# A gated Toeplitz convolution in fp32: units taken in pairs, a place of its own for each chunk of x, and another order of transfers in the last stretch

## The chip, the core and the metric

One NeuronCore of a Trainium2 chip runs the whole program. TensorE (PE in the profile) multiplies, ScalarE (ACT) and VectorE (DVE) empty PSUM and do the pointwise work, GpSimd (POOL) does pointwise work on SBUF, and SyncE (SP) issues every DMA of this kernel from one in-order queue. The metric is device time in microseconds, the median of three runs: 815.77 us before (814.77 to 816.03).

## What is computed

With x of shape (8, 64, 64, 96) in float32, `srms` dividing each token by the root of its mean square, and `toep1`, `toep2` the two causal-and-anticausal convolutions whose 127 coefficients per channel come from small networks of four layers (written as FFTs of double length in the reference):

```python
xn  = srms(x)
u   = silu(xn @ u_w.T + u_b)                  # 288 channels
v   = silu(xn @ v_w.T + v_b)                  # 288 channels
out = toep2(v, along rows) + toep1(v, along columns)
return (u * out) @ o_w.T + o_b + x
```

## The kernel before, in words

The 8 images are two halves of four. A half has 32 steps of 512 tokens. The program has five stages, in this order:

- **Phase A** (0 to about 175 us): for each step of half 0, the x of that step is scaled by its norm (`scale`, POOL), transposed (`transpose_x`, PE), split into a high and a low part (ACT, DVE), and multiplied by the two weight matrices (`project`, PE). ACT applies silu; v stays in SBUF, u is stored to DRAM by SP (`store_u`). x comes in 8 chunks of 4 steps (`load_x_all`). POOL squares a chunk two chunks ahead of its use (`square_a0`), DVE sums it and makes the norms. Chunks 0 to 3 lie in rows of v that are still free, chunks 4, 5, 6 in the three tiles `x_late`, and chunk 7 in the first of these again.
- **Phase C for half 0** (to about 325 us): the convolution, in 36 units of 8 channels. For unit n, PE transposes v into the PSUM banks 4 and 5 (`transpose_v`), multiplies along columns with 64x64 tiles (`along_columns`, 16 instructions, line 1034) and along rows with 128x128 tiles (`along_rows`, 8 instructions, line 1049). The sums of unit n lie in banks 0 and 1 for even n, 2 and 3 for odd n. ACT copies the transposed v to SBUF (`evacuate_vt`, line 591) and the result back into v (`evacuate_y`, lines 597 and 602). DVE writes the Toeplitz matrices of unit n + 2 from a staged tile that SP loads (`toeplitz`, lines 826 and 832; `load_stage`). In half 0 DVE also makes the norms of half 1 there.
- **Phase B0** (to about 538 us): the output of half 0, step by step, together with the projections of half 1.
- **Phase C for half 1** (to about 690 us).
- **Phase B1** (to the end): the output of half 1. For step t, SP has loaded u into one of four places (`load_u`), POOL multiplies it by the convolved v (`gate`, line 504), PE transposes the product in three parts (`transpose_g`, line 984) and, one step behind, multiplies by the output weights (`project_out`, lines 994 and 997), DVE adds x, which SP has loaded into the tile `x_e1` (`load_xe`, `add_x`), and SP stores that tile (`store_out`). `x_e1` has four places too.

Each engine runs its instructions in the order of the code, and waits on semaphores where one engine needs another. Two such waits matter below. `transpose_v(n)` waits for `vt_ready`, the copy of the unit before, since all units share banks 4 and 5; `along_columns(n)` waits for all three parts of `evacuate_y(n - 2)`. In phase B1 `load_xe` waits for `o_stored`, the landing of the store that last used its place.

Of the kernel before, what the change touches and what calls it, by code (L numbers as in the profile page):

```python
# [32 lines left out]
IMAGES, HEIGHT, WIDTH, E = 8, 64, 64, 96  # L33
D = 288
RPE, LAYERS = 256, 3
EPS = 1e-8
P = 128
H = P // 2
NB = 4
STEPS = HEIGHT // 2  # L40
# [3 lines left out]
NCH = 3  # L44
# [3 lines left out]
UNITS = D // UNIT  # L48
RC = RPE // P
TOK = NB * P  # L50
CH = 4
CHUNKS = STEPS // CH
PAIRS = 4
# [5 lines left out]
def tno_kernel(nc, x, x_eT, u_wT, u_b, v_wT, v_b, o_wT, o_b, pos_w, pos_b, lwT, lb, out_wT, out_b, out):  # L59
# [7 lines left out]
    with ctx:  # L67
# [3 lines left out]
        def place(name, shape, offset, dtype=f32):  # L71
            return nc.alloc_sbuf_tensor_at(name, shape, dtype, offset=base + offset)
# [6 lines left out]
        free_rows = place("free_rows", [P, D // 2, 2, P], 0)  # L79
# [4 lines left out]
        CHUNK_ROWS = CH * NB  # L84
# [3 lines left out]
        OB = OW + 2 * RC * NCH  # L88
        RH = OB + 2 * NCH
        RSQ, RIN, W_RAW = RH + 2 * RC, RH + 4 * RC, RH + 6 * RC  # L90
        assert W_RAW + 2 * NCH <= D // 2

        def lw_row(n, o, layer, c):
            return LW + ((n * RC + o) * LAYERS + layer) * RC + c
# [6 lines left out]
        V = V_BYTES  # L101
# [10 lines left out]

        g = place("g", [P, 5, TOK], V + 36864, f32r)
        g1 = [place(f"g1{k}", [P, 5, TOK], V + 26624 + 12288 * k, f32r) for k in range(2)]
        x_late = [place(f"x_late{k}", [P, CHUNK_ROWS, E], V + offset) for k, offset in enumerate((36864, 13824, 0))]

        def x_chunk(c):

            if c < FREE_CHUNKS:
                return rows(CHUNK_ROWS * c, CHUNK_ROWS, E)  # L120
            return x_late[(c - FREE_CHUNKS) % 3][:]

        x_n = place("x_n", [P, CH * NB, E], V + 22528)

# [108 lines left out]
        def _(sp):  # L233
# [10 lines left out]
            def load_x_all(c):  # L244
                wait(sp, x_all_loaded, 32 * c)
                for i in range(2):
                    sp.dma_start(x_chunk(c)[H * i:H * i + H], rows_of(0, CH * c, CH, i)).then_inc(x_all_loaded, 16)
# [50 lines left out]
            def load_xe(half, t, r):  # L298
                k = r % (2, CH)[half]
                sp.dma_start((x_e, x_e1)[half][:, k].rearrange("e (s m) -> e s m", s=2), tokens_of(x_eT, half, t)  # L300
                             ).then_inc(xe_loaded[half][k], 16)

            def store_out(half, t, r):
                k = r % (2, CH)[half]
                sp.wait_ge(o_ready, STEPS * half + t + 1)
                sp.dma_start(tokens_of(out, half, t), (x_e, x_e1)[half][:, k].rearrange("e (s m) -> e s m", s=2)
                             ).then_inc(o_stored[half][k], 16)
# [11 lines left out]
                                 ).then_inc(stage_loaded[k], 16)  # L319

            def phase_a(c, first, last):
                if c + 3 < CHUNKS - 1:
                    load_x_all(c + 3)
                elif c + 2 == CHUNKS - 1:

                    sp.wait_ge(x_scaled, CH * (c + 2 - 2))
                    load_x_all(c + 2)
                for r in range(CH):
                    if last and r == 2:
                        sp.wait_ge(a_stored, 32)  # L330
                        for n in range(2):
                            load_stage(0, n)
                    store_u(0, CH * c + r, u_tile(0, r), ua_stored[r % 2])
# [63 lines left out]
            def phase_b1():  # L397
                def body(c, first, last):
                    for r in range(CH):
                        t = CH * c + r  # L400
                        if not (first and r == 0) and not (last and r > 0):
                            sp.wait_ge(y_transposed, NCH * STEPS + NCH * t)
                            load_u(1, t + 3, r + 3)
                        if not (first and r < CH - 1) and not (last and r == CH - 1):
                            up = (r + 1) // CH
                            sp.wait_ge(o_stored[1][(r + 1) % CH], 16 * c + 16 * up)
                            load_xe(1, t + 1, r + 1)
                        if not first or r >= 2:
                            store_out(1, t - 2, r + 2)
                for c in range(CHUNKS):  # L410
                    body(c, c == 0, c == CHUNKS - 1)
                for t in range(STEPS - 2, STEPS):
                    store_out(1, t, t)
# [126 lines left out]
        def _(act):  # L540
# [45 lines left out]
            def phase_c(half):  # L586
                def evacuate_vt(n):
                    N = UNITS * half + n
                    act.wait_ge(vt_transposed, N + 1)
                    wait(act, conv_done, N - 1)  # L590
                    nc.scalar.copy(vt[n % 2][:], ps[:, VT_BANK:VT_BANK + 2].rearrange("p b (c m) -> p (b c) m", m=P)  # L591
                                   ).then_inc(vt_ready, 1)

                def evacuate_y(n):
                    act.wait_ge(conv_done, UNITS * half + n + 1)
                    bank, pair, pairs = SET_BANK[n % 2], UNIT // 2 * n, UNIT // 4
                    nc.scalar.copy(v[:, pair:pair + pairs],  # L597
                                   ps[:, bank].rearrange("p (c e m) -> p c m e", e=2, m=P)).then_inc(conv_out, 1)

                    for i in range(2):  # L600
                        to, of = slice(H * i, H * i + H), slice(H - H * i, P - H * i)
                        nc.scalar.copy(v[to, pair + pairs:pair + 2 * pairs],  # L602
                                       ps[of, bank + 1].rearrange("p (c e m) -> p c m e", e=2, m=P)
                                       ).then_inc(conv_out, 1)

                evacuate_vt(0)
                for n in range(UNITS):
                    if n:
                        evacuate_y(n - 1)
                    if n + 1 < UNITS:  # L610
                        evacuate_vt(n + 1)
                    elif half == 0:
                        high_x(STEPS, 0)
                evacuate_y(UNITS - 1)

            def body0(c, first, last):
                for r in range(CH):
# [304 lines left out]
        def _(pe):  # L922
# [93 lines left out]
            def phase_c(half):  # L1016
                def transpose_v(n):
                    N = UNITS * half + n
                    wait(pe, vt_ready, N)
                    for c in range(UNIT):  # L1020
                        last = nc.tensor.transpose(ps[:, VT_BANK + c // NB, (c % NB) * P:(c % NB + 1) * P],  # L1021
                                                   v[:, UNIT // 2 * n + c // 2, :, c % 2], (ident, swap)[c // NB][:])
                    last.then_inc(vt_transposed, 1)
# [27 lines left out]
                                                start=False, stop=True, skip_group_check=True)  # L1051
                    last.then_inc(conv_done, 1)

                pe.wait_ge(silu_done, PAIRS * STEPS * (half + 1) - 2)
                transpose_v(0)
                for n in range(UNITS):
                    if n < 2:
                        pe.wait_ge(silu_done, PAIRS * STEPS * (half + 1) - 1 + n)
                    along_columns(n)
                    if n + 1 < UNITS:  # L1060
                        transpose_v(n + 1)
                    elif half == 0:
                        transpose_x(STEPS, 0)
                    along_rows(n)

            def body0(c, first, last):
                for r in range(CH):
# [83 lines left out]
```

## Time and profile before

| | |
|---|---|
| median of 3 runs | 815.77 us (814.77 to 816.03) |
| profiled execution | 814.11 us |
| its span | 812.3 us |
| PE busy | 749.5 us (92%) |
| ACT, DVE, POOL busy | 533.9, 470.2, 282.6 us |
| granted TensorE clock, mean | 0.989 |
| DMA queue of SP | 160.15 MB, 70.6% of 16 engines |

The span goes from the first instruction to the last; the device time of the same execution is 1.8 us longer. Busy time says little here by itself: a stage in which PE is busy all the time and a stage in which a transfer sets the pace lie next to each other, and the page's forty slices of 20.3 us show it (PE reads 9 tenths in nearly all of them, and 8 or 7 in most of the last six, which are phase B1). "Idle before, released by" behind an instruction names what it waited for last.

### The profile page before, as it was taken

Reading aid. Unit: us, or ns where it says so; the run is one execution under the profiler, and the core shown is the slowest. Engines: PE = TensorE matmul, PEld = TensorE weight load, DVE = VectorE, ACT = ScalarE, POOL = GpSimd, SP = SyncE. Lnnn points to the kernel's source line nnn. Section 1 sums busy time; section 2 is a strip of 40 time slices with the busy share of each in tenths; the row PEclk is TensorE's granted clock in tenths of the full one; section 3 lists DMA queues with packets and bytes.
Section 4 is the critical chain, followed back from the end, with each engine's and each line's share of the span. In section 5 each row is a group of like instructions: output and inputs, shape, how many; then the busy total and the mean of one; then the engine's idle time right before and its main releaser. Section 6 shows DMA issues by size and latency. Waiting matters only on the chain.

```text
span 812.3 us, 19208 instructions
## 1 busy us (share of the span) xinstructions
PE 749.5 (92%) x7148; PEld 672.2 (83%) x7148; DVE 470.2 (58%) x845; ACT 533.9 (66%) x866; POOL 282.6 (35%) x187
## 2 busy tenths in 40 slices
PE   0999997998999999899999999989999998987887
PEld 0999886988999998799999999979999998765655
DVE  6566542336898886444444454445455553776666
ACT  0566574775666666677777877746666666655554
POOL 4333333212212112655555555410000001966764
PEclk9999998999999999999999999989999999999999
DMA  9555554369889786488988888776555555688786
GB/s 209 159 156 156 156 134 138 160 199 215 187 193 200 160 187 191 144 272 272 270 271 262 266 275 271 231 202 144 133 134 131 136 134 185 200 250 248 247 262 193
DMA packets 132017, 161.11 MB, mean 198 GB/s; under 512 B 69484, under 2 KB 97132, under 8 KB 131948
## 3 DMA queue, kind: packets, MB, share of 16 engines
q1 hardware_dynamic: 131948, 160.15, 70.6%
q8 instruction: 48, 0.79, 0.4%
q14 instruction: 21, 0.17, 0.1%
HBM read 109.49 MB, written 50.63 MB: 197 GB/s over the span
## 4 chain that ended last, share of the span: by engine, by line
PE 75%; DMA 13%; DVE 4%; issue 2%; POOL 2%; SPq 2%; ACT 1%; ACTq 0%; DVEq 0%; POOLq 0%
PE ps L974 22%; PE ps L1049 15%; PE ps L1021 9%; PE ps L1034 9%; DMA out<-x_e 9%; PE ps L994 7%; PE ps L984 6%; PE ps L965 3%; DMA stage<-a_dram 2%; PE ps L997 1%; POOL u_in L504 1%; DMA u_dram<-u_in 1%; SPq L300 1%; PE ps L948 1%; DMA free_rows<-in_x 1%
## 5 line engine op out<-in xcount | busy, mean ns | idle before, releaser
L504 POOL TENSOR_TENSOR u_in<-u_in,v 128x1152 f32<-128x1152 f32 (+2 forms) x66 | 174.6, 2651 | 177.5 <-DMA u_in<-u_dram 161.0
L876 DVE TENSOR_TENSOR g<-ps,g 128x512 fp32r<-128x512 f32 (+1 forms) x192 | 125.7, 681 | 74.9 <-ACT g L571 45.8
L832 DVE COPY toepB<-stage 64x512 f32<-64x512 f32 x144 | 105.2, 730 | 80.1 <-PE ps L1049 72.6
L1049 PE MATMUL ps<-toepB,vt 128*128 128x128 f32 x1152 | 141.8, 277 | 0.9 <-POOL toepB L488 0.5
L1049 PEld LDWEIGHTS ps<-toepB,vt 128*128 128x128 f32 x1152 | 136.3, 194 | 1.4 <-POOL toepB L488 0.7
L974 PE MATMUL ps<-wu,xh 97*128 97x288 f32 x512 | 123.6, 307 | 2.1
L766 DVE TENSOR_TENSOR xl<-ps,xh 96x512 fp32r<-96x512 f32 x64 | 43.9, 687 | 140.5 <-ACT xh L544 140.5
L974 PE MATMUL ps<-wv,xh 97*128 97x288 f32 x512 | 120.8, 311 | 2.3 <-ACT u_in L548 1.3
L984 PE MATMUL ps<-ident,u_in 128*128 128x128 f32 (+1 forms) x768 | 102.2, 276 | 21.3 <-POOL u_in L504 20.3
L984 PEld LDWEIGHTS ps<-ident,u_in 128*128 128x128 f32 (+1 forms) x768 | 81.7, 127 | 36.8 <-DVE g L876 12.7
L548 ACT ACTIVATE v<-ps 128x576 f32 (+1 forms) x128 | 83.5, 652 | 38.2 <-PE ps L974 28.7
L994 PE MATMUL ps<-g,wo 128*96 128x512 f32 x384 | 101.8, 400 | 0.0
L567 ACT CAST g<-ps 128x512 fp32r<-128x512 f32 x128 | 68.9, 590 | 47.8 <-PE ps L984 47.6
L591 ACT COPY vt<-ps 128x1024 f32<-128x1024 f32 x72 | 72.9, 1012 | 39.8 <-PE ps L1021 39.8
L974 PEld LDWEIGHTS ps<-wu,xh 97*128 97x128 f32 x512 | 89.1, 190 | 11.3 <-issue 3.7
L974 PEld LDWEIGHTS ps<-wv,xh 97*128 97x128 f32 x512 | 88.0, 193 | 3.5 <-ACT u_in L548 1.6
L548 ACT ACTIVATE u_out<-ps 128x576 f32<-128x576 f32 x96 | 62.6, 652 | 41.3 <-PE ps L974 39.5
L1034 PE MATMUL ps<-v,toepA 64*64 64x128 f32 x2304 | 82.9, 280 | 5.6 <-DVE toepA L826 5.6
L602 ACT COPY v<-ps 64x512 f32<-64x512 f32 x144 | 83.6, 581 | 3.6
L597 ACT COPY v<-ps 128x512 f32<-128x512 f32 x72 | 42.2, 586 | 59.0 <-PE ps L1049 59.0
L1034 PEld LDWEIGHTS ps<-v,toepA 64*64 64x64 f32 x2304 | 64.8, 132 | 14.4 <-issue 4.0
L974 PE MATMUL ps<-wv,xl 97*128 97x288 f32 x256 | 76.7, 300 | 0.0
(79 smaller groups left out, 1006.5 us busy)
## 6 DMA issues: line engine op xcount, KB each, us to landing
stage<-a_dram SPq DMA_DIRECT2D x144, 256.0 KB, 4.3
u_in<-u_dram SPq DMA_DIRECT2D x64, 576.0 KB, 5.3
u_dram<-u_out SPq DMA_DIRECT2D x48, 576.0 KB, 3.3
x_e<-in_x_eT SPq DMA_DIRECT2D x64, 192.0 KB, 3.8
out<-x_e SPq DMA_DIRECT2D x64, 192.0 KB, 3.8
u_dram<-u_in SPq DMA_DIRECT2D x16, 576.0 KB, 2.8
x_n<-in_x SPq DMA_DIRECT2D x16, 384.0 KB, 5.4
xa<-in_x SPq DMA_DIRECT2D x64, 96.0 KB, 4.6
```

What stands on the lines that cost most here:

```text
L504: return nc.gpsimd.tensor_tensor(out=tile, in0=tile, in1=v[:, start // 2:end // 2, bass.ds(t * NB, NB)].rearrange("p c n e -> p n c e"), o ...
L548: nc.scalar.activation(target, source, ACT.Silu).then_inc(silu_done, 1)
L591: nc.scalar.copy(vt[n % 2][:], ps[:, VT_BANK:VT_BANK + 2].rearrange("p b (c m) -> p (b c) m", m=P)).then_inc(vt_ready, 1)
L602: nc.scalar.copy(v[to, pair + pairs:pair + 2 * pairs], ps[of, bank + 1].rearrange("p (c e m) -> p c m e", e=2, m=P)).then_inc(conv_out, 1)
L832: nc.vector.tensor_copy(toepB[n % 2][rows, :, rows], stage[n % STAGES][rows, axis].rearrange("p k c -> p c k")[:, :, ::-1]).then_inc(toepB ...
L876: nc.vector.tensor_tensor(out=low, in0=ps[0:w, bank], in1=high.bitcast(f32), op=ALU.subtract).then_inc(gl_ready, 1)
L974: last = nc.tensor.matmul(ps[:, n, 0:D], (xh, xl)[xp][r % 2][:, n * P:(n + 1) * P], w[:, wp], start=(k == 0), stop=(k == len(SPLIT) - 1))
L984: last = nc.tensor.transpose(columns[:, n // 2, n % 2], u_in[:, r % CH, n, k * P:k * P + KW[k]], ident[:])
L994: nc.tensor.matmul(ps[0:E, bank], wo[:, 2 * k + wp], tile[:, 2 * k + gp], start=(k + s == 0), stop=False)
L1021: last = nc.tensor.transpose(ps[:, VT_BANK + c // NB, (c % NB) * P:(c % NB + 1) * P], v[:, UNIT // 2 * n + c // 2, :, c % 2], (ident, swap ...
L1034: last = nc.tensor.matmul(ps[to, SET_BANK[n % 2] + b, c * P:(c + 1) * P], toepA[n % 2][of, ch], v[of, UNIT // 2 * n + ch // 2, :, ch % 2], ...
L1049: last = nc.tensor.matmul(ps[:, SET_BANK[n % 2] + c // NB, (c % NB) * P:(c % NB + 1) * P], vt[n % 2][:, c], toepB[n % 2][:, c], start=Fals ...
```

## The change

Three edits, with no instruction of arithmetic added or taken away.

1. **Phase C.** PE takes the units two by two: both `along_columns`, then for each of the two `along_rows` and `transpose_v` of the unit two further on. The first two transposes come ahead of everything, and the wait for the last silus is one wait before them. ACT begins with two `evacuate_vt` and then alternates `evacuate_y(n)`, `evacuate_vt(n + 2)`.
2. **Phase A.** Chunk 4 of x goes to another free region of rows of v, chunks 5, 6, 7 to the three `x_late` tiles. No place is used twice, the wait on `x_scaled` is gone, and chunk 7 is loaded at the start of chunk 4, where before it was loaded at the start of chunk 5.
3. **Phase B1.** In the body of step t SP issues the load of u(t + 3), then the store of the output t - 2, then the load of x(t). Before it was u(t + 3), x(t + 1), output t - 2.

```diff
         def x_chunk(c):
             if c < FREE_CHUNKS:
                 return rows(CHUNK_ROWS * c, CHUNK_ROWS, E)
-            return x_late[(c - FREE_CHUNKS) % 3][:]
+            if c == FREE_CHUNKS:
+                return free_rows[:, X_FREE:X_FREE + CHUNK_ROWS, 1, P - E:P]
+            return x_late[c - FREE_CHUNKS - 1][:]
...
             def phase_a(c, first, last):
-                if c + 3 < CHUNKS - 1:
+                if c + 3 < CHUNKS:
                     load_x_all(c + 3)
-                elif c + 2 == CHUNKS - 1:
-                    sp.wait_ge(x_scaled, CH * (c + 2 - 2))
-                    load_x_all(c + 2)
...
                             load_u(1, t + 3, r + 3)
-                        if not (first and r < CH - 1) and not (last and r == CH - 1):
-                            up = (r + 1) // CH
-                            sp.wait_ge(o_stored[1][(r + 1) % CH], 16 * c + 16 * up)
-                            load_xe(1, t + 1, r + 1)
                         if not first or r >= 2:
                             store_out(1, t - 2, r + 2)
+                        if not first:
+                            sp.wait_ge(o_stored[1][r], 16 * c)
+                            load_xe(1, t, r)
...
-                evacuate_vt(0)
+                for n in range(2):
+                    evacuate_vt(n)
                 for n in range(UNITS):
-                    if n:
-                        evacuate_y(n - 1)
-                    if n + 1 < UNITS:
-                        evacuate_vt(n + 1)
-                    elif half == 0:
+                    evacuate_y(n)
+                    if n + 2 < UNITS:
+                        evacuate_vt(n + 2)
+                    elif half == 0 and n == UNITS - 2:
                         high_x(STEPS, 0)
-                evacuate_y(UNITS - 1)
...
-                pe.wait_ge(silu_done, PAIRS * STEPS * (half + 1) - 2)
-                transpose_v(0)
-                for n in range(UNITS):
-                    if n < 2:
-                        pe.wait_ge(silu_done, PAIRS * STEPS * (half + 1) - 1 + n)
-                    along_columns(n)
-                    if n + 1 < UNITS:
-                        transpose_v(n + 1)
-                    elif half == 0:
-                        transpose_x(STEPS, 0)
-                    along_rows(n)
+                pe.wait_ge(silu_done, PAIRS * STEPS * (half + 1))
+                for n in range(2):
+                    transpose_v(n)
+                for n in range(0, UNITS, 2):
+                    for k in range(2):
+                        along_columns(n + k)
+                    for k in range(2):
+                        along_rows(n + k)
+                        if n + 2 + k < UNITS:
+                            transpose_v(n + 2 + k)
+                        elif half == 0 and k == 0:
+                            transpose_x(STEPS, 0)
```

TensorE inside phase C, before. `toepA` belongs to the products along columns, `toepB` and `vt` to those along rows, `ident` and `swap` to the transposes; x16, x8 and x4 are instructions in a row.

```order
L1034 MATMUL ps<-v_49,toepA1_72 64x128 x16
L1021 MATMUL ps<-ident_90,v_49 128x128 x4
L1021 MATMUL ps<-swap_91,v_49 128x128 x4
L1049 MATMUL ps<-toepB1_74,vt1_76 128x128 x8
L1034 MATMUL ps<-v_49,toepA0_71 64x128 x16
L1021 MATMUL ps<-ident_90,v_49 128x128 x4
L1021 MATMUL ps<-swap_91,v_49 128x128 x4
L1049 MATMUL ps<-toepB0_73,vt0_75 128x128 x8
```

And after the change, at the same place:

```order
L1032 MATMUL ps<-v_49,toepA0_71 64x128 x16
L1032 MATMUL ps<-v_49,toepA1_72 64x128 x16
L1047 MATMUL ps<-toepB0_73,vt0_75 128x128 x8
L1019 MATMUL ps<-ident_90,v_49 128x128 x4
L1019 MATMUL ps<-swap_91,v_49 128x128 x4
L1047 MATMUL ps<-toepB1_74,vt1_76 128x128 x8
L1019 MATMUL ps<-ident_90,v_49 128x128 x4
L1019 MATMUL ps<-swap_91,v_49 128x128 x4
```

Two units have two groups of 64x64 products in both; after the change these stand together, and the products along rows of the first unit have a transpose and the rows of the second right behind them.

SyncE in phase A, from the middle on, before. `x_late0` is the place of chunk 7, `a_dram` takes the convolution's coefficients.

```order
L277 DMA a_dram<-r_a_78 128x36x8 [waits a_ready]
L277 DMA a_dram<-r_a_78 128x36x8
L295 DMA u_dram<-u_in_51 128x1152 [waits silu_done]
L295 DMA u_dram<-u_out_60 128x1152 [waits silu_done]
L295 DMA u_dram<-u_in_51 128x1152 [waits silu_done]
L295 DMA u_dram<-u_out_60 128x1152 [waits silu_done]
L247 DMA x_late0_64<-in_x 64x16x96 [waits x_all_loaded,x_scaled]
```

After the change chunk 7 is in `x_late2`:

```order
L281 DMA a_dram<-r_a_78 128x36x8 [waits a_ready]
L281 DMA a_dram<-r_a_78 128x36x8
L251 DMA x_late2_66<-in_x 64x16x96 [waits x_all_loaded]
L251 DMA x_late2_66<-in_x 64x16x96
L299 DMA u_dram<-u_in_51 128x1152 [waits silu_done]
L299 DMA u_dram<-u_out_60 128x1152 [waits silu_done]
L299 DMA u_dram<-u_in_51 128x1152 [waits silu_done]
```

The load moved ahead of four stores of u; it now stands between the store of the coefficients and the store of u of step 16.

SyncE in phase B1, before, for a little more than a step. The digit at the end of `o_stored` is the place in `x_e1`.

```order
L306 DMA out_0<-x_e1_53 96x2x256 [waits o_ready]
L290 DMA u_in_51<-u_dram 128x1152 [waits y_transposed]
L300 DMA x_e1_53<-in_x_eT 96x2x256 [waits o_stored10]
L306 DMA out_0<-x_e1_53 96x2x256 [waits o_ready]
L290 DMA u_in_51<-u_dram 128x1152 [waits y_transposed]
```

And after:

```order
L294 DMA u_in_51<-u_dram 128x1152 [waits y_transposed]
L310 DMA out_0<-x_e1_53 96x2x256 [waits o_ready]
L304 DMA x_e1_53<-in_x_eT 96x2x256 [waits o_stored13]
L294 DMA u_in_51<-u_dram 128x1152 [waits y_transposed]
L310 DMA out_0<-x_e1_53 96x2x256 [waits o_ready]
```

The load of x before waited for the store issued one step earlier (t + 1 and t - 3 share a place); now it waits for the store issued two steps earlier (t and t - 4 share one).

## Rows read from the trace of the kernel before

**Rows 1.** Windows; columns: stretch, length, busy PE, PEld, DVE, ACT, POOL, PEclk, DMA share, GB/s.
```profile
375.00:380.00 5.00, 5.00 (x35) 4.54 (x35) 3.02 (x5) 3.78 (x7) 3.38 (x2) 1.00 1.01 325
340.00:540.00 200.00, 198.24 (x1420) 180.84 (x1418) 94.23 (x149) 156.61 (x271) 99.51 (x58) 1.00 0.83 258
713.00:788.00 75.00, 60.89 (x371) 44.67 (x369) 51.82 (x79) 41.45 (x80) 50.77 (x20) 1.00 0.80 251
```

**Rows 2.** Timeline of SyncE in phase B1: start, length, instruction (all us).
```profile
717.11 0.45 SPq L306 DMA_DIRECT2D out<-x_e  x1
...
720.81 0.32 SPq L300 DMA_DIRECT2D x_e<-in_x_eT  x1
721.17 0.45 SPq L306 DMA_DIRECT2D out<-x_e  x1
```

**Rows 3.** Timeline of PE in phase B1, the output products.
```profile
698.39 1.64 PE L994 MATMUL ps<-g,wo 128*96 128x512 f32 x6
...
701.33 1.64 PE L994 MATMUL ps<-g,wo 128*96 128x512 f32 x6
...
805.37 1.64 PE L994 MATMUL ps<-g,wo 128*96 128x512 f32 x6
```

**Rows 4.** Transfers issued from 713 to 788 us: count, size, median us to landing.
```profile
u_in<-u_dram SPq DMA_DIRECT2D x19, 576.0 KB, 5.5
x_e<-in_x_eT SPq DMA_DIRECT2D x20, 192.0 KB, 3.4
```

**Rows 5.** Timeline of PE in phase A; in brackets idle time before it and releaser.
```profile
116.53 0.40 PE L974 MATMUL ps<-wv,xh 97*128 97x288 f32 x1 [1.32 <-ACT u_in L548]
...
120.47 0.38 PE L974 MATMUL ps<-wv,xh 97*128 97x288 f32 x1
...
129.81 1.09 PE L965 MATMUL ps<-ident,xa 128*96 128x128 f32 x4 [5.61 <-POOL xa L443]
...
136.25 0.38 PE L974 MATMUL ps<-wv,xh 97*128 97x288 f32 x1
```

**Rows 6.** Timeline of POOL in phase A.
```profile
128.14 0.83 POOL L456 TENSOR_TENSOR x_sq<-x_late 128x384 f32<-128x384 f32 x1 [15.70 <-DMA x_late<-in_x]
```

**Rows 7.** Timeline of SyncE in phase A.
```profile
108.22 3.38 SPq L295 DMA_DIRECT2D u_dram<-u_in  x1
...
121.43 1.60 SPq L247 DMA_DIRECT2D x_late<-in_x  x2
```

**Rows 8.** Timeline of ACT in phase A.
```profile
115.82 1.19 ACT L548 ACTIVATE u_in<-ps 128x576 f32<-128x576 f32 x2 [2.18 <-DMA u_dram<-u_in]
```

**Rows 9.** Timeline of PE's weight loads over one unit of phase C.
```profile
603.02 1.88 PEld L1049 LDWEIGHTS ps<-toepB,vt 128*128 128x128 f32 x16
605.02 0.89 PEld L1034 LDWEIGHTS ps<-v,toepA 64*64 64x64 f32 x32
606.09 0.55 PEld L1021 LDWEIGHTS ps<-ident,v 128*128 128x128 f32 x4 [0.18 <-issue]
...
607.03 0.31 PEld L1049 LDWEIGHTS ps<-toepB,vt 128*128 128x128 f32 x2
```

**Rows 10.** Timeline of ACT over the same unit.
```profile
605.13 0.59 ACT L597 COPY v<-ps 128x512 f32<-128x512 f32 x1 [0.77 <-PE ps L1049]
605.74 1.19 ACT L602 COPY v<-ps 64x512 f32<-64x512 f32 x2
607.35 1.01 ACT L591 COPY vt<-ps 128x1024 f32<-128x1024 f32 x1 [0.42 <-PE ps L1021]
```

**Rows 11.** Timeline of PE where the phases C and B1 start.
```profile
190.74 1.14 PE L1034 MATMUL ps<-v,toepA 64*64 64x128 f32 x32 [1.78 <-DVE toepA L826]
...
542.10 1.98 PE L1034 MATMUL ps<-v,toepA 64*64 64x128 f32 x32 [3.86 <-DVE toepA L826]
...
690.92 2.19 PE L984 MATMUL ps<-ident,u_in 128*128 128x128 f32 x12 [2.51 <-POOL u_in L504]
```

**Rows 12.** Timeline of DVE in phase C of half 0.
```profile
231.55 3.78 DVE L832 COPY toepB<-stage 64x512 f32<-64x512 f32 x2 [0.76 <-PE ps L1049]
```

More of the change, by code:

```diff
@@ L90, in tno_kernel @@
         RSQ, RIN, W_RAW = RH + 2 * RC, RH + 4 * RC, RH + 6 * RC
-        assert W_RAW + 2 * NCH <= D // 2
+        X_FREE = W_RAW + 2 * NCH
+        assert X_FREE + CHUNK_ROWS <= D // 2
         def lw_row(n, o, layer, c):
@@ L114, in tno_kernel @@
         g1 = [place(f"g1{k}", [P, 5, TOK], V + 26624 + 12288 * k, f32r) for k in range(2)]
-        x_late = [place(f"x_late{k}", [P, CHUNK_ROWS, E], V + offset) for k, offset in enumerate((36864, 13824, 0))]
+        x_late = [place(f"x_late{k}", [P, CHUNK_ROWS, E], V + offset) for k, offset in enumerate((0, 13824, 36864))]
         def x_chunk(c):
```

## The prediction, made before the changed kernel had run

> **What bounds the kernel now.** I read the windows by stage first. In phase B0 TensorE is busy 198.24 of 200 us, in phase B1 60.89 of 75 us, and no other engine is full there [rows 1]. So the stages differ, and each edit has to be priced in its own stage.
>
> Phase B1: SP's timeline shows what sets the step. The store of one output is issued at 717.11, the next load of x at 720.81, and 0.36 us later the next store, at 721.17 [rows 2]. The load of x waits for the landing of the store before it, the next store stands behind the load of x, so store, landing (3.7 us), load, store is a circle of 4.06 us a step. The output products of TensorE show the same: 698.39 to 701.33, or 2.94 us a step, while the places are still full, but 104.04 us for the 28 steps from 701.33 to 805.37, 3.72 us a step [rows 3].
>
> Phase A: TensorE idles 5.61 us ahead of the transpose at 129.81 [rows 5], since POOL waited 15.70 us for chunk 7 of x [rows 6], which SP issued only at 121.43 [rows 7].
>
> Phase C: TensorE is never idle over the unit shown. From 603.02 to 607.03 its weight loads follow each other, 4.01 us a unit [rows 9], while ACT waits 0.77 and 0.42 us [rows 10].
>
> **Phase B1, step by step.** The work of a step on TensorE is unchanged, so its floor is 2.94 us. The load of x now waits for the store issued two steps earlier. The old circle then spans two steps and no longer binds: 3.7 us of landing in two steps. Is there another circle? The load of x of step t goes out behind the store of t - 2; it must land (3.4 us in the median [rows 4], from 713 to 788), DVE adds, the store of t goes out, then the load of t + 2: about 3.4 + 1.3 us for two steps, 2.35 a step; even with 5 us of landing it is 3.15. For u: transposes of t - 1 done, u lands 5.5 us later [rows 4], then POOL's gate and the transposes of t + 3, some 10.2 us in four steps, 2.55 a step. Neither circle binds before the data rate does. A step moves 576 KB of u, 192 KB of x and 192 KB of output, 983,040 bytes. At 2.94 us this would be 334 GB/s. B1 runs at 251 GB/s with a DMA share of 0.80; B0 holds 258 GB/s over 200 us, where TensorE sets the pace, and its best 5 us move 325 GB/s at a share of 1.01 [rows 1]. So the pace comes out between 2.94 us (TensorE) and 3.81 us (258 GB/s), and nearest to the row in which the engines were full: 325 GB/s gives 3.02, with some gaps I take 312 GB/s, 3.15 us. The first five steps stay at 2.94 us as the places are full. Then 5 x 2.94 + 23 x 3.15 = 87.2 us in place of 104.0, a gain of **16.9 us**; bounds 1.7 (3.81 us) and 21.7 (2.94 throughout). The last load of x goes out a step later than before, but the last products of TensorE hide most of its landing, so I put nothing for it.
>
> The Trainium skill (DMA: Bandwidth & Descriptors, Specifications) gives a limit from HBM of about 358 GB/s for a core. By it the step would need 2.75 us of transfer and TensorE would set the pace, with the full 21.7 us; no row here shows such a rate over 5 us.
>
> **Phase A.** A step of four projections takes 3.94 us when nothing waits (116.53 to 120.47); the two steps from 120.47 to 136.25 took 15.78 us [rows 5], the lower clock after the idle time included. With chunk 7 loaded a chunk earlier the whole 7.9 us go. But the load moves to a bad place: right behind the store of the coefficients in runs of 32 bytes, which holds up the issue of the next store of u for 3.38 us [rows 7]. That store lands late already: ACT waits 2.18 us for it at 115.82 [rows 8], and TensorE 1.3 us behind ACT [rows 5]. Now 384 KB of x stand ahead of it. At least this costs nothing, at most the 3.4 us that the store was held up; I take 1.5 us. Then TensorE idles 3 us there. At 690.92 an idle time of 2.51 us was followed by 12 transposes in 2.19 us [rows 11]. Four transposes of phase C have their weight loads done in 0.55 us [rows 9], so 12 take some 1.5 at the higher level: the granted clock had fallen from 2.4 to 1.2 GHz. In phase A the lower level after 129.81 makes 7.9 us out of 5.61 us of idle time, 2.3 us more; after a shorter idle time I add 1.7 us. Phase A gains 7.9 - 1.5 - 1.7 = **4.7 us**; bounds 7.9 - 3.4 - 1.7 = 2.8 and 7.9.
>
> **Phase C.** A unit has one change from 128x128 to 64x64 products and one back. Weight loads of the row products start every 0.113 us (1.88 us for 16, the last one's own 0.19 off), so without a change the next would start at 603.02 + 1.80; it starts at 605.02, 0.20 later [rows 9]. The 32 loads of the 64x64 products need 0.80 us by their own spacing, and the transpose starts 1.07 after the first, 0.27 later [rows 9]. Taken by two, one such pair of changes goes in every two units: 8.03 becomes 7.56 us.
>
> But ACT now comes into the circle. Let the row products of unit n start at 0. ACT's copy of the result starts 2.11 later (603.02 to 605.13) and ends at 3.91; the copy of vt takes 1.01, so the banks of the transposes are free at 4.95 [rows 9, 10]. TensorE wants them for the transpose of n + 3 at 1.80 + 0.94 + 1.80 = 4.54, since two row products and one transpose are all that lies between. Before, a whole unit lay between. So it waits 0.44 us: 5.0 + 0.94 (transpose) + 0.20 + 2 x 0.80 + 0.27 = 8.0 us for two units in place of 8.03. The other new wait, of the second column products for the second copy of the result, ends at 6.8 where TensorE arrives at 6.9, and costs nothing. The saving of the changes is eaten by the wait. I take 7.98; the spacing of the 64x64 loads leaves 7.87 to 8.10.
>
> The rest of phase C: the last pair of a half needs no transpose and keeps its saving, 1.1 us in half 1 and 0.9 in half 0. At the start of half 0 the matrix of unit 3 isn't ready until 190.74 [rows 11], and in the new order the row products of unit 2 stand behind this wait instead of ahead of it: -2.2 us. In half 1 the transposes of unit 1 move into the wait that ends at 542.10 [rows 11], which pays for the later start. DVE in half 0 is nearly full, and its matrix for unit n + 3 now has 2.8 us of room where it had 5.8; a pair of its copies sometimes takes 3.78 us [rows 12] and eats most of it: -1 us. Sum: 31 x 0.05 + 2.0 - 2.2 - 1.0 = **+0.4 us**; bounds -5 (8.10 and more waits on DVE) and +5 (7.87).
>
> The Trainium skill (TensorEngine Tiling (Array Packing), Tiling Modes) says that changing the tiling mode drains TensorE. The gaps of 0.20 and 0.27 us agree. By that rule alone the edit would be worth 36 x 0.47 = 17 us; it doesn't look at who empties PSUM.
>
> **Sum.** 16.9 + 4.7 + 0.4 = 22.0 us against the profiled execution: 814.1 - 22.0 = 792.1. The median of the runs is 1.7 above that execution, so 793.7.
>
> **The rivals.**
> - TensorE sets the pace of B1, 2.94 us a step. For it: the circles above leave room, and single stretches reach 325 GB/s. Against it: 334 GB/s would have to hold for 80 us. It gives 793.7 - 4.8 = 788.9.
> - The transfers give less: with small packets of x and output between the large ones they stay near 270 GB/s, 3.6 us a step. For it: B0 averages 258 GB/s. Against it: there TensorE set the pace. 14.7 + 82.8 us is a gain of only 6.5: 804.1.
> - The pairs save all their changes of mode, 7.56 us for two units, because the wait on vt doesn't show. 31 x 0.42 = 13 us more: 780.7. Against it stands ACT's timeline.
> - The load of chunk 7 doesn't help, because POOL and DVE are late by themselves: 793.7 + 4.7 = 798.4. Against it: POOL idles 15.70 us there.
> - Slower: DVE becomes the bound of phase C in half 0. Its copies of the matrices come in the order rows n, columns n + 3, rows n + 3, with the norms between them; if a stretched copy (3.78 us) delays the columns of unit n + 3 in most pairs, TensorE waits up to 1.5 us in each of 17 pairs, and all later pairs inherit it. It takes 22 us, 1.3 us a pair, to undo the rest; at 1.5, 25.5 us: 819.2. Against it: in the rows POOL's long squares, which go with the stretched copies, come once in four units.
>
> **How the numbers follow.** Forecast 0.60, TensorE sets the pace 0.14, less from the transfers 0.12, all changes saved 0.06, chunk 7 without effect 0.04, slower 0.04. The forecast's 793.7, with the pace of B1 from 3.02 to 3.3 us and phase C at its bounds, covers about 787 to 800. The range of 783 to 806 takes in the rivals but the slower one and most of the one with all changes saved. Faster than before by over 0.2% (about 1.6 us, what a measurement can tell from no change) 0.93; within it 0.03, where the slowest end of the transfers meets the worst of phase C; slower 0.04.
>
> **What the profile of the changed kernel would show.** In B1 SP no longer waits for a landed store ahead of the load of x, the output products start every 3.0 to 3.3 us, the DMA share is over 0.9 and the rate over 300 GB/s. In phase A no idle time of TensorE near 124 us, a longer one near 115. In phase C two units take 8.0 us, and the second transpose of each pair waits about 0.4 us for the copy of vt. I am wrong if the B1 rate stays under 280 GB/s, if TensorE is full there, or if two units take under 7.8 or over 8.3 us.

## The result

| | before | after |
|---|---|---|
| median | 815.27 us (4 runs, 812.87 to 816.03) | 791.81 us (4 runs, 791.14 to 794.66) |
| profiled execution | 814.11 us | 791.14 us |
| its span | 812.3 us | 789.3 us |
| PE busy | 749.5 us (92%) | 740.7 us (94%) |
| DMA queue of SP | 160.15 MB, 70.6% | 160.15 MB, 72.2% |

The ratio is 0.9724, with a 95% interval of 0.9692 to 0.9756. The forecast was 793.7 us. It came within 1.9 us, but two of its three terms were off, in opposite directions, and the runs below sort them out.

I cut each profiled execution at four places: the start of the last product of phase A, the end of the last row products of each phase C, and the start of the last output product of phase B0. That gives the length of each stage in us (rounded one by one).

| | A | C0 | B0 | C1 | B1 and end | span |
|---|---|---|---|---|---|---|
| before | 174.8 | 148.5 | 213.7 | 151.5 | 123.9 | 812.3 |
| after | 170.1 | 151.3 | 213.8 | 151.8 | 102.5 | 789.3 |
| gain | 4.7 | -2.8 | -0.1 | -0.2 | 21.4 | 23.0 |
| predicted | 4.7 | -1.5 | 0 | 1.9 | 16.9 | 22.0 |

(The prediction gave phase C as one sum, 0.4; its terms are put to their halves here.)

### The profile page after: what moved, and what is told of

It is laid out like the page before. It is cut to its first block, busy times and chain, and to the rows that moved or that the text cites. A ratio compares the mean times of both kernels' runs of the same rounds, so it can differ in the third digit from the quotient of the medians.

```text
span 789.3 us, 19203 instructions
## 1 busy us (share of the span) xinstructions
PE 740.7 (94%) x7148; PEld 672.7 (85%) x7148; DVE 472.6 (60%) x845; ACT 530.2 (67%) x866; POOL 280.6 (36%) x187
## 3 DMA queue, kind: packets, MB, share of 16 engines
q1 hardware_dynamic: 131948, 160.15, 72.2%
## 4 chain that ended last, share of the span: by engine, by line
PE 74%; ACT 11%; issue 4%; DMA 4%; DVE 4%; POOL 1%; SPq 1%; POOLq 0%; ACTq 0%; DVEq 0%
PE ps L972 24%; PE ps L992 10%; PE ps L982 10%; PE ps L1047 9%; PE ps L1032 9%; ACT v L601 5%; PE ps L1019 5%; ACT vt L590 4%; PE ps L963 3%; PE ps L995 2%; DMA stage<-a_dram 2%; POOL u_in L503 1%; DMA u_in<-u_dram 1%; DMA u_dram<-u_in 1%; PE ps L946 1%
## 5 line engine op out<-in xcount | busy, mean ns | idle before, releaser
L503 POOL TENSOR_TENSOR u_in<-u_in,v 128x1152 f32<-128x1152 f32 (+2 forms) x66 | 174.6, 2653 | 155.0 <-DMA u_in<-u_dram 137.7
L1047 PE MATMUL ps<-toepB,vt 128*128 128x128 f32 x1152 | 144.9, 279 | 0.0
L830 DVE COPY toepB<-stage 64x512 f32<-64x512 f32 x144 | 99.7, 693 | 55.9 <-PE ps L1047 48.9
L972 PE MATMUL ps<-wv,xh 97*128 97x288 f32 x512 | 119.0, 308 | 5.3 <-ACT u_in L547 4.0
L982 PEld LDWEIGHTS ps<-ident,u_in 128*128 128x128 f32 (+1 forms) x768 | 83.5, 128 | 13.4 <-ACT v L601 2.7
L1032 PE MATMUL ps<-v,toepA 64*64 64x128 f32 x2304 | 76.2, 279 | 2.4 <-DVE toepA L824 2.4
L824 DVE COPY toepA<-stage 128x512 f32<-128x512 f32 x72 | 48.5, 674 | 46.8 <-PE ps L1032 28.9
L972 PE MATMUL ps<-wu,xl 97*128 97x288 f32 x256 | 76.1, 297 | 0.0
```

Of the source, the lines that this page charges most:

```text
L503: return nc.gpsimd.tensor_tensor(out=tile, in0=tile, in1=v[:, start // 2:end // 2, bass.ds(t * NB, NB)].rearrange("p c n e -> p n c e"), o ...
L830: nc.vector.tensor_copy(toepB[n % 2][rows, :, rows], stage[n % STAGES][rows, axis].rearrange("p k c -> p c k")[:, :, ::-1]).then_inc(toepB ...
L972: last = nc.tensor.matmul(ps[:, n, 0:D], (xh, xl)[xp][r % 2][:, n * P:(n + 1) * P], w[:, wp], start=(k == 0), stop=(k == len(SPLIT) - 1))
L982: last = nc.tensor.transpose(columns[:, n // 2, n % 2], u_in[:, r % CH, n, k * P:k * P + KW[k]], ident[:])
L1032: last = nc.tensor.matmul(ps[to, SET_BANK[n % 2] + b, c * P:(c + 1) * P], toepA[n % 2][of, ch], v[of, UNIT // 2 * n + ch // 2, :, ch % 2], ...
L1047: last = nc.tensor.matmul(ps[:, SET_BANK[n % 2] + c // NB, (c % NB) * P:(c % NB + 1) * P], vt[n % 2][:, c], toepB[n % 2][:, c], start=Fals ...
```

## The profile after

Windows of the changed kernel (stretch, length, busy PE, PEld, DVE, ACT, POOL, PEclk, DMA share, GB/s), two stretches of 5 us in phase A and one of 75 us in B1:

```profile
115.00:120.00 5.00, 1.54 (x9) 1.54 (x10) 0.55 (x1) 1.98 (x4) 0.00 (x0) 0.95 0.71 265
120.00:125.00 5.00, 5.00 (x30) 4.99 (x30) 2.13 (x3) 2.90 (x6) 3.06 (x4) 0.71 0.24 99
...
700.00:775.00 75.00, 75.00 (x483) 60.15 (x482) 66.52 (x103) 53.77 (x103) 68.05 (x26) 1.00 1.00 325
```

The last row answers to the last of [rows 1]. TensorE was busy 60.89 of 75 us and is now busy for all 75; the rate went from 251 to 325 GB/s. So in this trace B1 isn't bound by its transfers, as I had forecast, but by TensorE.

**Phase B1.** The output products in TensorE's timeline:

```profile
731.95 1.64 PE L992 MATMUL ps<-g,wo 128*96 128x512 f32 x6
...
734.89 1.64 PE L992 MATMUL ps<-g,wo 128*96 128x512 f32 x6
...
737.83 1.64 PE L992 MATMUL ps<-g,wo 128*96 128x512 f32 x6
```

SyncE's timeline in the same stretch:

```profile
732.06 0.32 SPq L310 DMA_DIRECT2D out<-x_e  x1
732.43 0.45 SPq L304 DMA_DIRECT2D x_e<-in_x_eT  x1
732.92 0.48 SPq L294 DMA_DIRECT2D u_in<-u_dram  x1
734.95 0.32 SPq L310 DMA_DIRECT2D out<-x_e  x1
```

The step is 2.94 us, the floor of TensorE read from [rows 3]. The load of x goes out 0.37 us after the store ahead of it, where it stood 3.7 us behind before [rows 2]. SyncE's waits over B1 say it for the whole stretch (line, what it waited for, us in total, times, longest). Before, from 700 to 800 us:

```profile
SPq L300 <- DMA out<-x_e: 66.1, 26, 3.0
```

And after, from 700 to 775 us:

```profile
SPq L310 <- DVE x_e L883: 38.1, 25, 2.1
SPq L294 <- PE ps L982: 0.9, 2, 0.5
```

Before, 26 loads of x waited for a landed store, 2.5 us each. After, none does: SyncE waits for DVE to finish an output.

**Phase A.** The stall at chunk 7 is gone, and one near 115 us is longer. TensorE's timeline there, after the change:

```profile
118.46 0.40 PE L972 MATMUL ps<-wv,xh 97*128 97x288 f32 x1 [3.98 <-ACT u_in L547]
```

ACT's timeline, the instruction that TensorE waited for:

```profile
117.76 1.19 ACT L547 ACTIVATE u_in<-ps 128x576 f32<-128x576 f32 x2 [4.84 <-DMA u_dram<-u_in]
```

And SyncE's, ahead of it:

```profile
103.35 4.14 SPq L281 DMA_DIRECT2D a_dram<-r_a  x2
107.53 4.16 SPq L251 DMA_DIRECT2D x_late<-in_x  x2
111.73 0.97 SPq L299 DMA_DIRECT2D u_dram<-u_in  x1
```

The two loads of chunk 7 now stand where the store of u stood before, right behind the store of the coefficients, and take 4.16 us to issue, as that store took 3.38 [rows 7]; further on in the queue, in [rows 7], two such loads take 1.60. The store of u stands behind them. ACT goes on at 117.76, 1.9 us later than at 115.82 [rows 8], and TensorE's idle time grows from 1.32 to 3.98 us. The granted clock is at 0.71 of full speed from 120 to 125 us, a mix of its two levels, 1.2 and 2.4 GHz.

**Phase C.** TensorE's weight loads over a pair of units:

```profile
601.82 1.86 PEld L1047 LDWEIGHTS ps<-toepB,vt 128*128 128x128 f32 x16 [0.18 <-issue]
...
604.55 1.88 PEld L1047 LDWEIGHTS ps<-toepB,vt 128*128 128x128 f32 x16
606.79 0.56 PEld L1019 LDWEIGHTS ps<-ident,v 128*128 128x128 f32 x4 [0.37 <-ACT vt L590]
...
607.95 1.81 PEld L1032 LDWEIGHTS ps<-v,toepA 64*64 64x64 f32 x64
609.93 0.74 PEld L1047 LDWEIGHTS ps<-toepB,vt 128*128 128x128 f32 x6 [0.18 <-issue]
```

ACT's timeline beside them:

```profile
603.91 0.59 ACT L596 COPY v<-ps 128x512 f32<-128x512 f32 x1 [2.54 <-PE ps L1047]
604.52 1.18 ACT L601 COPY v<-ps 64x512 f32<-64x512 f32 x2
605.73 1.01 ACT L590 COPY vt<-ps 128x1024 f32<-128x1024 f32 x1
```

A pair takes 609.93 - 601.82 = 8.11 us, and two units took 8.02 [rows 9]. The wait on the copy of vt is there, 0.37 us long (0.44 was forecast): ACT ends that copy at 606.74, and the second transpose of the pair starts at 606.79.

## The experiments

Ten kernels ran. Ratios are to the kernel before on the same chip, with 95% intervals. Distances from the changed kernel are differences of medians that were taken at different times; taken from the ratios they differ by up to 2 us, so smaller ones say little. Where it matters the lengths of the stages are given too.

**Which edit brings what.** `e1_b1_only` is the kernel before with edit 3 alone, `e2_pairs_only` with edit 1 alone, and `e3_no_pairs` is the changed kernel with edit 1 undone. The core of e1 (e2 and e3 add and take away the last two pieces of the diff of the change):

```diff
-                        if not (first and r < CH - 1) and not (last and r == CH - 1):
-                            up = (r + 1) // CH
-                            sp.wait_ge(o_stored[1][(r + 1) % CH], 16 * c + 16 * up)
-                            load_xe(1, t + 1, r + 1)
...
+                        if not first:
+                            sp.wait_ge(o_stored[1][r], 16 * c)
+                            load_xe(1, t, r)
```

> The kernel before with the third edit alone (order of SP in phase B1). Theory: the circle store, landing, load of x, store is gone and TensorE sets the pace, 2.94 us a step; 812.3 - 21.4 = 790.9 us of span, ratio 0.974. Rival (the forecast's own: the transfers set the pace at 312 GB/s): 3.15 us a step, 795.4 us of span. Rival (part of the gain in B1 comes from the stages ahead of it): less than 20 us.

> The kernel before with the first edit alone (units of the convolution in pairs). Theory: a pair takes 8.11 us instead of 8.03 and the start of phase C in half 0 is later; 3 us slower, ratio 1.004. Rival (forecast): 0.4 us faster, ratio 1.000. Rival (the pairs gain, and what phase C lost in the changed kernel comes from chunk 7's place or the shifted phase A): ratio below 0.999.

> The changed kernel with the first edit undone: the units one by one as before, with both other edits. Theory: 3 us faster than the changed kernel, span 786, ratio to before 0.968. Rival: 0.4 us slower than the changed kernel, ratio 0.973.

Measured: e1 791.07 us (0.9684, 0.9657 to 0.9711), e2 820.01 (1.0041, 1.0027 to 1.0054), e3 789.21 (0.9667, 0.9644 to 0.9691). Edit 3 alone brings 25 us, all that the change brings (22.2 between the two traces, 19.9 of them in B1 and the end). Edit 1 alone makes the kernel slower by 3.3 us (by the ratio), and leaving it out of the change makes that 2.6 us faster by the medians, 4.6 by the ratios. The stages say the same. The five kernels in this study with edit 1 and nothing else new in phase C (after, e2, e4, e5, e9) need 302.6 us for C0 and C1 together in the mean, the three without it (before, e1, e3) 299.8: edit 1 costs 2.8 us. Cut once more inside phase C, at the ends of the row products of the third pair of units, of the 17th and of the last (means, us), the traces show where:

| | C0: to the third pair | next 14 pairs | last pair | C1: to the third pair | next 14 pairs | last pair |
|---|---|---|---|---|---|---|
| without edit 1 | 29.48 | 112.37 | 7.44 | 31.04 | 112.37 | 7.07 |
| with edit 1 | 30.04 | 113.59 | 7.59 | 30.64 | 113.59 | 7.16 |

The columns of 14 pairs are the same to 0.05 us in all traces of a row: 8.11 us a pair against 8.03. So 2.4 of the 2.8 us are the 28 pairs in the middle.

For edit 2 the end of phase A tells more than the medians: 174.8, 174.6 and 173.1 us without it (before, e2, e1) against 170.1, 170.7, 170.1, 171.3, 171.4 and 171.9 with it (after, e3, e4, e6, e7, e9), a gain of 3.2 us between the means. Single traces with the same code up to there differ by almost 1.9 us, and the clock goes with it: from 115 to 125 us its mean is 0.83 of full speed in after and e4 (both 170.1) and 0.66 in e3, e6, e7 and e9 (170.7 to 171.9). The 4.7 us come from one of the two traces with the higher clock.

**Order or distance in B1.** In `e4_x_first` the load of x stands ahead of the store, but still waits for the store of two steps earlier.

```diff
-                        if not first or r >= 2:
-                            store_out(1, t - 2, r + 2)
                         if not first:
...
                             load_xe(1, t, r)
+                        if not first or r >= 2:
+                            store_out(1, t - 2, r + 2)
```

> The changed kernel with one thing altered in phase B1: SP issues u(t + 3), then x(t), then the store of t - 2; the load of x still waits for the store of t - 4, issued two steps earlier. Theory: the distance to the store that is waited for matters, not the order of the two transfers; 2.94 us a step, the same time as the changed kernel, ratio 0.972. Rival: the order matters (stores ahead of loads); the pace goes back towards 3.7 us and the span to 805 or more.

Measured: 792.55 us (0.9709, 0.9674 to 0.9744). Its window:

```profile
720.00:770.00 50.00, 49.95 (x315) 38.55 (x312) 42.92 (x67) 35.38 (x68) 44.33 (x17) 1.00 1.05 320
```

The window of the changed kernel over the same stretch:

```profile
720.00:770.00 50.00, 50.00 (x324) 40.19 (x323) 44.26 (x69) 35.76 (x69) 45.97 (x18) 1.00 1.03 333
```

TensorE is full in both. SyncE's waits of e4 from 700 to 775 us show that it does wait for landed stores again:

```profile
SPq L304 <- DMA out<-x_e: 31.6, 23, 1.9
SPq L310 <- DVE x_e L883: 12.4, 15, 1.6
```

They are shorter, 1.4 us each where they were 2.5 before, and nearly fit into the step: the 30 steps of e4 take 3.01 us in the mean, against 2.96 in the changed kernel, 3.66 in the kernel before and 2.97 to 3.17 in the seven other kernels with edit 3 and no added bytes. The rival had put e4 back towards 3.7. What counts is how many steps lie between a store and the load that waits for it; what the order of the two adds can't be told from the scatter.

**How near the transfers are to being the bound.** `e9_more_bytes` adds one load of 192 KB a step to B1, into memory nobody reads, 20% more bytes.

```diff
+                        if not first:
+                            wait(sp, junk_loaded[t % 2], 16 * ((t - CH) // 2))
+                            sp.dma_start(junk[:, t % 2].rearrange("e (s m) -> e s m", s=2), tokens_of(x_eT, 1, t)
+                                         ).then_inc(junk_loaded[t % 2], 16)
```

> The changed kernel; in phase B1 SP issues one more load of 192 KB per step from step 4 on, into a place that nobody reads, so a step moves 1,179,648 bytes instead of 983,040. Theory: 333 GB/s in B1 is TensorE's pace and close to what the transfers can give, so with 20% more bytes they set the pace: 3.45 to 3.6 us a step, 28 steps, 14 to 18 us slower than the changed kernel, ratio to before 0.989 to 0.995. Rival (there is room left): up to 400 GB/s at 2.94 us a step, the same time as the changed kernel.

Measured: 809.49 us (0.9949, 0.992 to 0.9979), 17.7 us slower than the changed kernel by the medians; its ten runs lie between 806.48 and 816.59. Its window:

```profile
720.00:785.00 65.00, 56.78 (x344) 41.29 (x343) 45.84 (x72) 37.98 (x73) 48.46 (x19) 1.00 1.06 329
```

The loads of u in that stretch (count, size, median us from issue to landing):

```profile
u_in<-u_dram SPq DMA_DIRECT2D x18, 576.0 KB, 7.3
```

And in the changed kernel, from 720 to 770 us:

```profile
u_in<-u_dram SPq DMA_DIRECT2D x17, 576.0 KB, 5.7
```

With more bytes the rate doesn't rise over the 333 GB/s of after: it is 329, TensorE idles 13% of the stretch, and the loads of u land 1.6 us later. It isn't a new circle in the queue: in this stretch SyncE waits 18 times for DVE and 15 times for TensorE, and never for a landing. So here the transfers do set the pace, and 1,179,648 bytes at 329 GB/s are 3.59 us a step; 18 loads in 65 us are 3.61. The changed kernel needs 983,040 bytes in 2.94 us, 334 GB/s, and gets it. It sits right at the edge: TensorE needs 2.94 us a step, and 983,040 bytes at the 329 to 333 GB/s of the two windows take 2.95 to 2.99. The Trainium skill (DMA: Bandwidth & Descriptors, Specifications) gives about 358 GB/s for a core. Its direction was right, TensorE does set the pace, and my 312 was too low; but this case reached 325 to 333 over 50 us and more, not 358.

**Chunk 7 away from the short runs.** `e5_x7_early` is the changed kernel with the load of chunk 7 issued ahead of the coefficients' store, and that store split over two steps.

```diff
-                if c + 3 < CHUNKS:
+                if c + 3 < CHUNKS and c != LAYERS + 1:
...
+                    if c == LAYERS + 1 and r < 2:
+                        store_a(r)
...
-                    store_a()
+                    load_x_all(c + 3)
```

> The changed kernel; in phase A SP issues the load of chunk 7 ahead of the store of the coefficients, and the two halves of that store one step apart, each just ahead of a store of u. Theory: the 3.98 us of idle time of TensorE ahead of 118.46 and the lower clock after it come from the store of u that stands behind both; they go, and phase A ends 4 to 5.5 us sooner; some 1 to 2 us of it may be lost again at the start of phase C, which waits for loads. Ratio to before 0.966 to 0.968. Rival: another engine is late there (POOL, DVE) and TensorE waits for it instead; ratio as for the changed kernel, 0.972.

Measured: 791.33 us (0.9698, 0.9676 to 0.972), no difference by the medians, where 4 to 5.5 us were expected. TensorE's timeline at the stall:

```profile
116.28 0.61 PE L974 MATMUL ps<-wv,xh 97*128 97x288 f32 x1 [2.04 <-ACT u_in L549]
```

The window around it:

```profile
115.00:120.00 5.00, 3.72 (x15) 3.72 (x16) 2.35 (x2) 2.65 (x5) 0.24 (x1) 0.59 0.83 243
```

The idle time went from 3.98 to 2.04 us, but the granted clock fell all the same, to a mean of 0.59 over these 5 us. The split store holds the issue behind each of its halves instead of once: the two stores of u behind them take 4.54 and 3.38 us to issue, so the cost is moved more than removed. Phase A ended at 169.3, 170.0 and 168.2 us in the three kernels with this edit (e5, e8, e10), against 170.9 in the mean of the six that have edit 2 without it, so it is worth about 1.7 us there, as little as the traces can tell.

**The wait on vt taken away.** `e6_vt_banks` is the changed kernel with the transposed v of odd units in PSUM banks 6 and 7, which are free in phase C (the two `pe.wait_ge` that this takes at the ends of the phase, and one copy of DVE moved ahead, are not shown).

```diff
-        VT_BANK = 4
+        VT_BANK = [4, 6]
...
-                    wait(pe, vt_ready, N)
+                    wait(pe, vt_ready, N - 1)
```

> The changed kernel; the transposes of v use PSUM banks 4 and 5 for even units and 6 and 7 for odd ones (and DVE adds the last x of half 0 ahead of the first matrix of half 1, so that bank 7 is free). Nothing else. Theory: the wait of 0.4 us in each pair for the copy of vt goes, but ACT's second copy of the result then ends 0.2 us after TensorE wants it; a pair takes 7.9 us instead of 8.11, 34 pairs, 7 us faster than the changed kernel. Rival (only the wait on vt matters): 7.7 us a pair, 14 us faster. Rival (the pair is bound elsewhere): no change.

Measured: 786.0 us (0.9638, 0.9618 to 0.9657), 5.8 us faster than the changed kernel. TensorE's weight loads:

```profile
604.72 0.89 PEld L1032 LDWEIGHTS ps<-v,toepA 64*64 64x64 f32 x32
605.77 0.92 PEld L1032 LDWEIGHTS ps<-v,toepA 64*64 64x64 f32 x32 [0.17 <-issue]
606.87 1.86 PEld L1047 LDWEIGHTS ps<-toepB,vt 128*128 128x128 f32 x16 [0.18 <-ACT vt L590]
```

The transpose no longer waits, but the second group of column products now starts 0.17 us late: ACT's copies of the results alternate with the copies of vt, and the last part of the copy that it waits for ends at 605.66, 0.11 us before it starts. A pair takes 7.84 us. `e7_rows_first` takes e6 and puts both row products ahead of both transposes, and in ACT both copies of results ahead of both copies of vt:

```diff
                     evacuate_y(n)
-                    if n + 2 < UNITS:
-                        evacuate_vt(n + 2)
...
+                    evacuate_y(n + 1)
+                    for k in range(2):
+                        if n + 2 + k < UNITS:
+                            evacuate_vt(n + 2 + k)
...
                         along_rows(n + k)
-                        if n + 2 + k < UNITS:
-                            transpose_v(n + 2 + k)
...
+                    for k in range(2):
+                        if n + 2 + k < UNITS:
+                            transpose_v(n + 2 + k)
```

> As the kernel with two places for the transposes, and TensorE does both row products of a pair before both transposes, ACT both copies of the result before both copies of vt. Theory: no wait is left, a pair takes TensorE's own 7.7 us; 14 us faster than the changed kernel in half 1, somewhat less in half 0 if DVE, which has some 15 us of work in four units there, gets in the way; ratio to before 0.956. Rival (the saved changes of mode were never there): a pair takes 8.0 or more.

Measured: 783.55 us (0.9599, 0.9579 to 0.9619). TensorE over a pair:

```profile
602.06 2.05 PE L1034 MATMUL ps<-v,toepA 64*64 64x128 f32 x64
604.04 3.84 PE L1049 MATMUL ps<-toepB,vt 128*128 128x128 f32 x32
607.72 0.64 PE L1021 MATMUL ps<-ident,v 128*128 128x128 f32 x4
...
609.73 0.46 PE L1034 MATMUL ps<-v,toepA 64*64 64x128 f32 x8
```

The pair takes 7.67 us with no idle time of the matmuls, and C0 and C1 are 146.4 and 145.4 us long, together 11.2 us less than in the changed kernel. The whole is 8.3 us faster, short of the 14 expected: in this trace phase A is 1.3 and B1 2.3 us longer than in that of the changed kernel. The Trainium skill (TensorEngine Tiling (Array Packing), Tiling Modes) says that a change of mode drains TensorE. By that rule alone pairing saves 0.47 us in two units, from 8.02 to 7.55; e7 has 7.67, so 0.35 of it is there once nobody waits for PSUM. Nearly all of the missing 0.12 lies in the column products: the two groups together take 604.04 - 602.06 = 1.98 us, against 2 x 1.07 apart [rows 9], a saving of 0.16 where 0.27 had been counted.

**All of it.** `e8_all` is e7 with the edit of e5. `e10_norms_later` also puts the first load of the norms behind that of matrix 3 at the start of C0:

```diff
-                    sp.wait_ge(ua_stored[1], 16 * (STEPS // 2))
-                    load_norms(0)
                 for n in range(STAGES, UNITS):
                     load_stage(half, n)
+                    if half == 0 and n == STAGES:
+                        sp.wait_ge(ua_stored[1], 16 * (STEPS // 2))
+                        load_norms(0)
```

> The last one (rows first, two places for the transposes) together with the early load of chunk 7 and the split store of the coefficients. Theory: both gains add, 3 to 5 us below the kernel with rows first; ratio to before 0.951. Rival: what phase A gains is lost at the start of phase C; the same time as with rows first.

> The kernel with all of it (rows first, two places for the transposes, early chunk 7, split store); at the start of phase C in half 0 SP issues the load of the first x for the norms behind that of matrix 3 instead of ahead of it. Theory: the column products of unit 3 wait for that matrix, whose load stands behind 1.4 us of issue and 384 KB; 1 to 2 us faster, ratio to before 0.952 to 0.954. Rival: DVE, which needs the squares at unit 2, holds up the next matrices; same or slower.

Measured: e8 778.51 us (0.9546, 0.9522 to 0.957), e10 777.55 (0.954, 0.9519 to 0.9562). Both beat the kernel before by 37 to 38 us and the changed one by 13 to 14. Of the 5.3 us between the traces of e7 and e8 only 1.4 lie in phase A, where the edit is; 1.5 lie in phase C and 2.4 in B1, where nothing was changed. e8 and e10 aren't told apart by their times. In its trace e10 has C0 2.5 us shorter than e8 (143.5 against 146.0), as expected of the edit, and B1 with the end 7.1 us longer (109.6 against 102.5), though nothing was changed there; that trace is of its slowest run, 781.51 us. Its window:

```profile
695.00:770.00 75.00, 71.83 (x455) 55.67 (x454) 60.43 (x95) 50.05 (x96) 63.38 (x24) 1.00 0.97 303
```

e8 has TensorE busy for 74.87 us and 316 GB/s there. In e10 the loads of u land after 6.3 us (median, 700 to 770 us), in e8 after 5.7. So B1 scatters with what the transfers give, as a stage at the edge would; what slows them in some executions stays open.

## Why the prediction was right, and where not

- **Phase B1, the term mis-sized.** I put 3.15 us a step and 16.9 us; it was 2.94, and the stage gained 21.4. The circle of store, landing, load and store was read rightly, and so was the floor. The step that failed is "with some gaps I take 312 GB/s": I took the best 5 us of a stretch in which TensorE set the pace, less some gaps, for what the transfers can do. TensorE at 2.94 us was my first rival, priced at 788.9; 21.4 is within 0.3 us of its 21.7. But the stage runs at the edge, and in the nine kernels with edit 3 and no added bytes a step takes 2.96 to 3.17 us, 3.02 in the mean. By the means of the stages, 125.2 us for before and e2 and 104.3 for the nine, the gain is 20.9.
- **Phase C, wrong in sign.** I put +0.4; edit 1 costs 2.8 us. The wait on vt was read rightly: rows to transpose takes 4.97 us where I had 5.0, and transpose to columns 1.16 where I had 1.14. Four terms failed. The column products of a pair, "2 x 0.80" and 0.27, were to take 1.87 us; they take 1.98 (607.95 to 609.93), in e7 too, where nothing waits. My own sum gave 8.0 to 8.01 us, of which I took 7.98; the pair takes 8.11, so in place of 31 x 0.05 = +1.6 the 28 pairs in the middle cost 2.4. The last pairs were to keep 2.0 us and lose 0.24, for the second transpose of the pair before, with its wait, still stands ahead of their products. The start of half 0 was to cost 2.2 and costs 0.6, and that of half 1 gains 0.4. DVE was to cost 1.0 in half 0 and costs nothing: the 14 pairs take 113.59 us in both halves. These add up to the -2.8.
- **Phase A, right by the traces, 4.7 us.** The stall goes, and one of 3.98 us (I had 3) takes part of it back, with the clock. Over nine kernels the gain is 3.2, so the term was probably 1.5 too large, and that the two traces give 4.7 is luck of the clock; it lies within my bounds of 2.8 to 7.9.
- **The total** was within 1.9 us since +4.5 in B1 and -3.4 in phase C nearly cancel, and that is luck: a forecast that fits by its sum is no proof of its terms. Inside phase C the errors cancelled in part as well. Of my signs of being wrong one came true, TensorE is full in B1. It needed e2 and e3 to see that the kernel is faster without the pairs as they were written, and e6 and e7 to see that the pairs were worth having.

## What to carry to other kernels

A store, its landing and a load that waits for it in one in-order queue set a step of their own length; put two steps between them and the circle goes, whatever the order in the queue. When instructions are grouped to save changes of mode, look at who empties the PSUM that the group shares: without banks of its own for each member the saving turned into a wait here, and without the emptying engine's work grouped in the same way only part of it was there (7.84 us a pair in e6, 7.67 in e7). And a rate measured where another engine set the pace is a lower bound of what the transfers can do; one run with more bytes shows how near the upper one is.

## What the runs showed of the hardware

- Transfers of 576 KB and 192 KB from DRAM and 192 KB to it in each step hold 325 GB/s for 75 us and 333 for 50; with more bytes the trace shows no more (329). Another execution of the same stage (e10) had 303 GB/s with TensorE idle for 4% of the time. The profile's DMA share reads 0.97 to 1.06 in these stretches, and 1.05 at 320 GB/s in e4, so near 1 it doesn't tell how many bytes are moved.
- The granted clock fell around an idle time of 2.04 us in phase A of e5 (0.59 in its window), and didn't fall at one of 1.32 us in the kernel before, whose window is:

```profile
115.00:120.00 5.00, 3.63 (x26) 3.20 (x25) 2.35 (x2) 3.44 (x6) 0.00 (x0) 1.00 0.46 185
```

- A store in runs of 32 bytes, 2 x 144 KB, takes 4.14 us to issue, and the DMA behind it takes 3.4 to 4.5 us to issue, be it a load of x (4.16) or a store of u (3.38, and 4.54 and 3.38 behind the halves in e5). Away from it a store of u takes 0.32 us and the two loads of x 1.60.
